# A fused conditional mixing and feed-forward kernel: its head rebuilt with a selector product, aggregation on VectorE per block, and other idle products

## The reference

```python
# x: (64, 32, 512), cond_128: (64, 128); K = 8 kernels
h = gelu(cond_128 @ W0 + b0)
h = gelu(h @ W1 + b1)
att = softmax(h @ W2 + b2)                        # (64, 8)
agg_w = einsum('bk,koi->boi', att, weight)        # one 32x32 matrix for each batch row
agg_b = att @ bias_k
hs = einsum('boi,bih->boh', agg_w, x) + agg_b[:, :, None]
routing = top_k(hs @ gate_w, 2)                   # over 8 logits; their two largest
shared = relu(hs @ up_w) ** 2 @ down_w            # 512 -> 1024 -> 512
routed = ((hs @ fc1_w) @ expert_w) * sum(routing) @ fc2_w
out = x + layernorm(shared + routed) * ln_gamma + ln_beta
```

## Time and profile before

| | us |
|---|---|
| median of 3 runs | 268.63 |
| lowest, highest | 267.57, 270.42 |
| span of the profiled execution | 266.2 |
| TensorE busy in it | 259.0 |
| VectorE, ScalarE, GpSimd busy | 154.9, 85.2, 44.6 |

### The profile page before, as it was taken

The page is one execution under the profiler, slowest core; times in us unless marked ns, Lnnn a source line. Parts: engine busy times, 40 slices in busy tenths (PEclk is TensorE's granted clock), DMA queues, the critical chain, the costliest instruction groups (busy, mean ns, idle before and its releaser), DMA issues.

```text
span 266.2 us, 3377 instructions
## 1 busy us (share of the span) xinstructions
PE 259.0 (97%) x1222; PEld 215.7 (81%) x1222; DVE 154.9 (58%) x268; ACT 85.2 (32%) x146; POOL 44.6 (17%) x42
## 2 busy tenths in 40 slices
PE   7999999999999999999999999999999999999991
PEld 7698888788888888888888888888888888778891
DVE  3686899974444954384544963384444963314454
ACT  4356994441111354241110354231110355211110
POOL 1000409101111800001111810001111700001111
PEclk9999999999999999999999999999999999999997
DMA  6973710400111240000111140000111100001111
GB/s 211 342 224 147 264 52 10 151 0 0 42 39 39 49 151 0 0 0 4 39 39 39 42 155 0 0 0 0 39 39 39 42 0 0 0 2 39 39 39 39
DMA packets 9132, 15.71 MB, mean 59 GB/s; under 512 B 634, under 2 KB 3578, under 8 KB 9122
## 3 DMA queue, kind: packets, MB, share of 16 engines
q1 hardware_dynamic: 9122, 15.57, 17.4%
HBM read 11.37 MB, written 4.20 MB: 58 GB/s over the span
## 4 chain that ended last, share of the span: by engine, by line
PE 95%; issue 2%; DVE 1%; POOLq 0%; POOL 0%; DVEq 0%
PE ps L774 26%; PE ps L776 26%; PE ps L775 26%; PE ps L760 6%; PE ps L714 2%; PE ps L719 2%; PE ps L838 1%; PE ps L840 1%; PE ps L746 1%; PE ps L850 1%; POOLq L80 0%; POOL rstd L378 0%; PE ps L755 0%; DVE stats L617 0%; DVE y_buf L615 0%
## 5 line engine op out<-in xcount | busy, mean ns | idle before, releaser
L774 PE MATMUL ps<-down_hi,sq_hi 128*128 128x512 f32 (+1 forms) x136 | 51.3, 377 | 0.0
L775 PE MATMUL ps<-down_lo,sq_hi 128*128 128x512 f32 (+1 forms) x136 | 51.2, 377 | 0.0
L776 PE MATMUL ps<-down_hi,sq_lo 128*128 128x512 f32 (+1 forms) x136 | 51.2, 377 | 0.0
L774 PE MATMUL ps<-h_hi,up_hi 128*128 128x512 f32 x128 | 50.3, 393 | 0.0
L776 PE MATMUL ps<-h_hi,up_lo 128*128 128x512 f32 x128 | 49.8, 389 | 0.0
L775 PE MATMUL ps<-h_lo,up_hi 128*128 128x512 f32 x128 | 49.8, 389 | 0.0
L378 POOL TENSOR_TENSOR rstd<-mv,half 128x1 f32<-128x1 f32 x16 | 15.7, 982 | 177.4 <-DVE mv L622 171.9
L456 ACT ACTIVATE relu_sq<-ps 128x512 f32<-128x512 f32 x32 | 19.1, 597 | 58.1 <-PE ps L776 44.2
L615 DVE TENSOR_TENSOR y_buf<-ps,y_buf 128x512 f32<-128x512 f32 x15 | 10.4, 691 | 45.9 <-PE ps L776 45.9
L589 DVE CAST sq_hi<-relu_sq 128x512 fp32r<-128x512 f32 x32 | 23.6, 737 | 20.9 <-ACT relu_sq L458 20.2
L473 ACT ACTIVATE y_buf<-ps,top 128x512 f32<-128x512 f32 x16 | 11.0, 689 | 69.2 <-PE ps L776 67.2
(11 more groups left out here) (105 smaller groups left out, 302.4 us busy)
## 6 DMA issues: line engine op xcount, KB each, us to landing
x_cur<-in_x_dram SPq DMA_DIRECT2D x4, 1024.0 KB, 5.5
out_dram<-late SPq DMA_DIRECT2D x15, 256.0 KB, 2.0
late<-in_up_w_dram SPq DMA_DIRECT2D x4, 512.0 KB, 10.0
late<-in_down_w_dram SPq DMA_DIRECT2D x4, 512.0 KB, 5.3
experts_sb<-in_experts_dram SPq DMA_DIRECT2D x1, 768.0 KB, 5.1
agg_b<-aggb_dram SPq DMA_DIRECT2D x1, 768.0 KB, 8.1
latents_sb<-in_latents_dram SPq DMA_DIRECT2D x1, 528.0 KB, 3.9
affine_sb<-in_affine_dram SPq DMA_DIRECT2D x1, 512.0 KB, 5.4
```

The costliest lines, as they stand in the source:

```text
L774: nc.tensor.matmul(dst, a_hi, b_hi, start=first, stop=False)
L775: nc.tensor.matmul(dst, a_hi, b_lo, start=False, stop=False)
L776: return nc.tensor.matmul(dst, a_lo, b_hi, start=False, stop=last)
```

## The change

Four things are changed in the head, and one in all blocks.

- The idle products load and move a 128x128 tile of ones (L757 of the new file), 37 of them instead of 26.
- The weights come with a strided load of 32 partitions on ScalarE's queue. VectorE transposes them in 32x32 blocks, one product with a repeated identity spreads them to 128 partitions, and VectorE copies them to `weight_T`. The attention is laid out by tile and spread to the same partitions by a product with a selector (ATT_P). Then VectorE multiplies the two (128x1024) and sums over k: that is the aggregate of one block, already on the partitions where `mix` needs it, so that four copies make `mix`.
- Block 0's bias is prepared by GpSimd and ScalarE and added by TensorE, as one product of ones with the bias parts into each mixing bank. `mix_bias` is gone from block 0; `h_hi` and `h_lo` are taken from PSUM.
- up_w is loaded in five pieces, the first ahead of x. The second and third mixing chunks move behind the first chunk of the up product, and two foldings move ahead of the mixing.
- The copies of the whole aggregate are gone. `next_aggregate(b)` on VectorE, behind the eight square splits of block b, computes the aggregate of block b + 1, and `next_mix` on GpSimd waits for it.

```diff
-    UPC = INT // 4
+    UP_COLS = [(0, 1), (1, 1), (2, 2), (4, 2), (6, 2)]
-    MIX0_BANK = [7, 4, 7, 4]
+    MIX0_BANK = [5, 4, 7, 5]
...
         @block.gpsimd
+            pool.wait_ge(bias_loaded, 16)
+            pool.wait_ge(attT_copied, 1)
+            nc.gpsimd.tensor_tensor(
+                att_bias.rearrange("k (b o) -> k b o", o=C),
+                att_T[:, 0:TOK // C].unsqueeze(2).to_broadcast([K2, TOK // C, C]),
+                bias_raw.unsqueeze(1).to_broadcast([K2, TOK // C, C]),
+                ALU.mult).then_inc(attb_ready, 1)
+            pool.wait_ge(attb_hi_ready, 1)
+            nc.gpsimd.tensor_tensor(bias_parts[LO, :], att_bias[LO, :], bias_parts[LO, :].bitcast(fp32),
+                                    ALU.subtract).then_inc(attb_lo_ready, 1)
...
-            pool.wait_ge(agg_act, 2 * G)
-            pool.wait_ge(agg_dve, 2 * G)
             def next_mix(b):
                 pool.wait_ge(mix_done, HC * (b + 1))
                 pool.wait_ge(xbeta_ready, b + 1)
+                pool.wait_ge(next_agg_ready, b + 1)
...
         @block.scalar
+            act.dma_start(weight_raw[:, :, :], weight_v).then_inc(weight_loaded, 16)
+            act.dma_start(bias_sb[:, :], kernels[0:K2, C * C:]).then_inc(bias_loaded, 16)
...
-            for q in (0, 1):
-                for g in range(G):
-                    nc.scalar.copy(mix_part(g, q), agg_src(q, g, TB)).then_inc(mix0_act, 1)
+            for g in (0, 1):
+                r = slice(g * C, (g + 1) * C)
+                nc.scalar.copy(mix[r, :, r], agg[r, 0:TB, :]).then_inc(mix0_act, 1)
...
         @block.vector
+            nc.vector.memset(idle[:, :].bitcast(mybir.dt.uint32), ONE_BITS).then_inc(dve_const, 1)
...
+            dve.wait_ge(weight_loaded, 16)
+            nc.vector.transpose(weight_t[:, :, :].rearrange("i k o -> i (k o)"),
+                                weight_raw[:, :, :].rearrange("o k i -> o (k i)")).then_inc(weight_t_ready, 1)
...
+            nc.vector.tensor_copy(weight_T[:, :, :], WEIGHT_T.rearrange("p (k o) -> p o k", o=C)
+                                  ).then_inc(weightT_copied, 1)
...
+            nc.vector.tensor_tensor(
+                first_terms, weight_T[:, :, :].unsqueeze(1).to_broadcast([P, TB, C, K]),
+                ATT_P[:, 0:TB, :].unsqueeze(2).to_broadcast([P, TB, C, K]), ALU.mult).then_inc(first_terms_ready, 1)
+            dve.wait_ge(first_terms_ready, 1)
+            nc.vector.tensor_reduce(agg[:, 0:TB, :], first_terms, AX.X, ALU.add).then_inc(first_agg_ready, 1)
...
+            def first_mix_low(c):
+                dve.wait_ge(h_hi_ready, c + 1)
+                nc.vector.tensor_tensor(h_lo[:, c, :], ps[:, MIX0_BANK[c], :], h_hi[:, c, :].bitcast(fp32),
+                                        ALU.subtract).then_inc(h_lo_ready, 1)
+
+            def next_aggregate(b):
+                if isinstance(b, int) and b == 0:
+                    dve.wait_ge(attP_copied, 1)
+                    dve.wait_ge(mix0_act, 2)
+                else:
+                    dve.wait_ge(mix_ready, G * b)
+                nc.vector.tensor_tensor(
+                    next_terms, weight_T[:, :, :].unsqueeze(1).to_broadcast([P, TB, C, K]),
+                    att_P[:, bass.ds((b + 1) * TB, TB), :].unsqueeze(2).to_broadcast([P, TB, C, K]),
+                    ALU.mult).then_inc(next_terms_ready, 1)
+                dve.wait_ge(next_terms_ready, b + 1)
+                nc.vector.tensor_reduce(agg[:, bass.ds((b + 1) * TB, TB), :], next_terms, AX.X, ALU.add).then_inc(next_agg_ready, 1)
...
-            for q in (2, 3):
-                for g in range(G):
-                    nc.vector.tensor_copy(agg_part(g, q), agg_src(q, g, NT)).then_inc(agg_dve, 1)
...
+            next_aggregate(0)
             latent_low(0)
...
         @block.tensor
-                    nc.tensor.matmul(IDLE, gate_hl[:, 0, :], gate_hl[:, 1:3, :], start=True, stop=True)
+                    nc.tensor.matmul(IDLE, idle[:, :], idle[:, :], start=True, stop=True)
...
-            for c in range(C // G):
-                last = nc.tensor.matmul(AGG[:, c, :], weight_parts[:, c * P:(c + 1) * P], att_parts[:, :],
-                                        start=True, stop=True)
...
+            def first_mix_chunk(c):
+                for t in range(TB):
+                    nc.tensor.matmul(ps[:, MIX0_BANK[c], t * P:(t + 1) * P], x_cur[:, t, c * P:(c + 1) * P],
+                                     mix[:, t, :], start=(t == 0), stop=False)
+                if c == 0:
+                    pe.wait_ge(attb_lo_ready, 1)
+                nc.tensor.matmul(ps[:, MIX0_BANK[c], :], ones[:, :], bias_parts,
+                                 start=False, stop=True).then_inc(mix_done, 1)
```

More of the change, by code:

```diff
@@ L41, in adaln_ffn_kernel @@
     K = mlp.shape[1] - NB - 2 * D - 2
-    SR = kernels.shape[0]
-    FIRST, LAST = slice(0, K), slice(SR - K, SR)
+    LO, K2 = slice(0, K), 2 * K
+    ONE_BITS = 0x3F800000
     INT = up_w.shape[1]
@@ L143, in adaln_ffn_kernel @@
         b1_sb = mlp_sb[:, NB + 2 * D + K + 1:NB + 2 * D + K + 2]
[L144 to L147, removed]
+        weight_raw = h_full[0:C, 0, 0:K * C].rearrange("o (k i) -> o k i", k=K)
+        weight_t = h_full[0:C, 1, 0:K * C].rearrange("i (k o) -> i k o", k=K)
+        repeat = sb("repeat", [C, G, C])
+        weight_T = sb("weight_T", [P, C, K])
+        bias_sb = sb("bias_sb", [K2, C + K])
+        bias_raw = bias_sb[:, 0:C]
+        idle = sb("idle", [P, P], f32r)
+        b2_sb = bias_sb[0:1, C:C + K]
+        sel_g = sb("sel_g", [NB, G])
+        sel = sb("sel", [NB, G, C])
+        in_tile = sb("in_tile", [NB, NT])
+        att_tiles = sb("att_tiles", [NB, NT, K])
+        att_P = sb("att_P", [P, NT, K])
         hid1 = sb("hid1", [D, NB])
@@ L165, in adaln_ffn_kernel @@
         logits = sb("logits", [P, TB, NE])
-        ones = sq_lo[0:2 * K, 1, 0:P]
+        ones = sq_lo[0:K2, 1, 0:P]
         half = sb("half", [P, 1])
@@ L172, in adaln_ffn_kernel @@
         H2 = ps[:, 4, 128:128 + NB]
[L173 to L177, removed]
+        LOGIT = ps[0:NB, 2, 0:K]
+        ATT_T = ps[0:K2, 4, 256:256 + NB]
+        ATT_P = ps[:, 3, 0:NT * K].rearrange("p (t k) -> p t k", k=K)
+        WEIGHT_T = ps[:, 5, 0:K * C]
+        IDLE = ps[:, 0, 0:P]
+        AGGB_ROWS = ps[0:NB, 2, 0:C]
         TOP = ps[:, TOP_BANK, 0:TB * 2 * NE].rearrange("p (t s n) -> p t n s", t=TB, s=2)
         Q = [ps[:, 6, :], ps[:, 7, :]]
[L182 to L192, removed]
         def shared(t):
@@ L205, in adaln_ffn_kernel @@
         mlp_loaded = sem("mlp_loaded")
-        kernels_loaded = sem("kernels_loaded")
+        weight_loaded = sem("weight_loaded")
+        bias_loaded = sem("bias_loaded")
         experts_loaded = sem("experts_loaded")
         x_loaded = sem("x_loaded")
-        up_loaded = [sem(f"up_loaded{i}") for i in range(4)]
+        up_loaded = [sem(f"up_loaded{i}") for i in range(len(UP_COLS))]
         latents_loaded = sem("latents_loaded")
@@ L688, in _ @@
                     split_square(b, m)
+                next_aggregate(b)
                 latent_low(b)
@@ new lines, in _ @@
+            nc.tensor.matmul(LOGIT, ones[0:1, 0:NB].bitcast(fp32), b2_sb, start=True, stop=False)
+            stay_warm(2)
+            pe.wait_ge(gelu_done, 2)
+            nc.tensor.matmul(LOGIT, hid2[:, :], w2_sb, start=False, stop=True).then_inc(logit_done, 1)
+            pe.wait_ge(weight_t_ready, 1)
+            pe.wait_ge(repeat_ready, 1)
+            nc.tensor.matmul(WEIGHT_T, repeat[:, :, :].rearrange("j g i -> j (g i)"),
+                             weight_t[:, :, :].rearrange("i k o -> i (k o)"),
+                             start=True, stop=True).then_inc(weightT_done, 1)
@@ L748, in _ @@
-            last.then_inc(agg_done, 1)
             pe.wait_ge(attT_copied, 1)
             nc.tensor.matmul(AGGB_ROWS, att_T[0:K, :], bias_raw[0:K, :], start=True, stop=True).then_inc(rows_done, 1)
-            stay_warm(1)
-            pe.wait_ge(attb_lo_ready, 1)
-            nc.tensor.matmul(AGG_B, ones[:, :], bias_parts, start=True, stop=True).then_inc(aggb_done, 1)
-            stay_warm(3)
+            fold_expert(0, 1, 0)
+            fold_expert(0, 1, 1).then_inc(q_done, 1)
+            stay_warm(6)
```

219 lines of the change are left out of this document (110 added, 109 removed).

## The result

The changed kernel took 278.77 us (median of 6, 275.60 to 280.77) against 268.75 (median of 6, 267.21 to 270.42). The ratio of the compared runs is 1.027, 95% interval 1.020 to 1.034. It is lower than the ratio of the medians because the comparison leaves out the three runs at 280.7 as disturbed; runs of two further kernels with this head, further down, fall into the same two groups, some 4 us apart. The prediction was 270.5 with a range of 266.3 to 272.6; all six times lie above it. The six times stand in groups: 275.6 twice, 276.84, and 280.7 three times. The profile is of one at 280.77, so it shows the worst group.

A forecast was written before the change was run, and what follows sets the result against it. TensorE, busy 259.0 of 266.2 us, was taken as the bound, so the head pays only by starting the up product earlier. Sum: 267.6 - 2.2 (head) + 3.5 (gap) + 0.1 (loop) + 1.5 (clock) = 270.5; range 266.3 to 272.6.

The forecast's parts named there:

- With the clock up: ... the up product starts at 15.4: Head, mixing to up product: at 2.4 GHz the first up product starts at 15.4 instead of 18.24 us, 2.8 earlier.
- the head's net gain of 2.2: Head: 2.8 us earlier start less 0.9 given back in the up product; 1.9, or 2.7 without GpSimd's hold; 2.2 taken.
- Idle products at 0.13, bound 0.19: Head start: twenty idle products at 0.13 us each by columns, at most 0.19; first real product at 3.5.
- Aggregate ready at 11.2, and the mixing on VectorE's chain: Head: VectorE's multiplication (1.26) and sum (1.2) end at 11.2 us; mixing follows its copies, at 11.9, or 12.8 if held.
- The clock up for the mixing: Head: TensorE at 2.4 GHz when mixing starts, so two chunks cost 0.11 us an instruction instead of 0.21.
- My rival for it: Head: idle products don't raise the clock; net gain only 0.5, total 270.7 to 272.2, about 271.6 us; chance 0.18.
- Bias product 0.23 each: Block 0 mixing: the bias becomes one 512-column product a chunk, 0.23 us each.
- GpSimd's hold of 0.8: Head: GpSimd's bias subtraction (1.2 us) holds VectorE's copies, so mixing starts at 12.8, gaining 0.8 instead of 1.7.
- The gap: End of block 0: TensorE waits 3.5 to 4.3 us, say 3.9, for the next aggregate and GpSimd's copies; net 3.5.
- The clock in the gap: Behind block 0's gap: the clock probably drops, costing 1.5 us (0 to 3.5); rival that it holds, 269.0, chance 0.25.
- The loop: Later blocks: aggregate and copies on time or slightly late, 0 to 0.3 us a block, 0.1 for both.

The follow-up runs named there:

- the early aggregate: Changed kernel with block 0's next_aggregate ahead of the eight square splits instead of behind: 273.86 us, ratio 1.016; control repeat 272.15, ratio 1.010.
- old idle products: Changed kernel with the idle products of before (96 columns of zero weights, 192 moved), 11 instead of 20 at the start: 272.71 us; with the early aggregate too, 269.53.
- old idle, 16 rows: Changed kernel with the early aggregate and the old idle products, bias products left at 16 rows: 269.53 us, ratio 0.999.
- 128 rows: Changed kernel with block 0's bias products padded from 16 to 128 rows: 276.55 us alone, 270.91 with the early aggregate.
- all three edits: Changed kernel with the early aggregate, the old idle products and bias products of 128 rows: 267.47 us, ratio 0.993.
- another kernel's: Changed kernel with only the bias products widened to 128 rows, gap and new idle products kept: 276.55 us, profiled execution 276.84.

## Why the prediction was wrong

**The step that failed is "With the clock up: ... the up product starts at 15.4", and with it the head's net gain of 2.2.** The second half started 8.2 us later instead of 2.2 earlier, 10.4 in all, where the profiled execution (280.77) missed the forecast by 10.3. The other terms nearly cancel: 0.9 less for gap and fall, 0.2 more in the other blocks, and 0.5 more outside the span. Of the 10.4, the mixing began 4.6 late (17.42 against 12.8), mixing to up product took 2.6 more (5.2), and the first half of the up product 2.9 more than the prediction's 14.9; the last 0.3 is the 2.2 taken where the terms gave 1.9. In the lower group too, with the clock up before the up product, the head is some 4 us late instead of 2.2 early (second half at 36.27 in the trace of the early aggregate, at 272.02). Its terms:

- *Idle products at 0.13, bound 0.19.* They cost 0.23. I let the price follow the columns moved and left the weights out; even my upper bound was too low. The mean weight load takes 0.33 us against 0.27 in the heads of the two kernels, and the products stand in the same ratio, 1.2; but no run varied the weights' columns alone, and the tile's values changed with them. H1 started at 5.6 instead of 3.5. In time: 2.6 us (269.53 against the lower group's 272.1), or 3.4 (267.47 against 270.91), the earlier rise of the clock included.
- *Aggregate ready at 11.2, and the mixing on VectorE's chain.* With H1 back at 3.56 (old idle products) the sum still ended at 12.7. I had left out the product that spreads the weights (L780, 1.15 us on the chain) and the four idle products behind it. The multiplication and the sum, 1.22 each, were right (1.26 and 1.2 predicted). And I never followed TensorE's own list to the mixing: it ended at 17.42, the copies at 16.80.
- *The clock up for the mixing.* Not so in this execution: low until 27.4. My rival for it priced only 1.1 us of mixing and no up product; a late rise cost 4.2.
- *Bias product 0.23 each.* That is the price at 128 rows. At 16 rows it was 0.43, and 0.2 more on what follows. The first half of the up product was 15.62 (old idle, 16 rows) and 14.80 (128 rows) instead of 13.97: 1.65 and 0.8 given back, where 0.9 was predicted.
- *GpSimd's hold of 0.8.* Right for the copies, 1.0 measured by taking it away, but the mixing waited for TensorE's list and not for them; its removal gained nothing.

Even with all three edits the second half starts at 32.03 against 32.21 in the profiled executions, 0.2 earlier and not 2.2; block 0's mixing, 2.84 instead of 3.26, is the rest of the 0.6 between their spans. By the medians that version gains 2.0 (267.47 against 269.47): the profiled execution of before, at 267.57, is one of its fastest. Where its slower ones lose their 1.9 us no trace shows.

**The gap was right in mechanism and near in size.** Predicted 3.9, measured 2.98. Shifted by the head's 10.4, TensorE was ready at 58.96 (58.8 predicted) and VectorE's last split ended at 57.96 (57.5 predicted). GpSimd's four copies took 1.33, not 2.3 to 2.95; that is most of the difference. That it costs 3.5 in all, without a fall of the clock, is shown by the early aggregate; gap and fall together cost 4.4 (276.3 to 280.7), 5.0 predicted.

**The clock in the gap** was put at 1.5. Against a mixing of 2.92 it cost 1.4 in the profiled execution, 2.5 in another kernel's, and nothing in the one with old idle products. The size was right as a middle, and the event is not certain.

**The loop** cost nothing (0.1 predicted); the other blocks are 0.3 longer.

The steps from all three edits (267.5) back to the lower group (275.6), 2.1 for the rows, 2.6 for the idle products and 3.5 for the gap, add up by construction. Two kernels outside that row test them: old idle products with the gap kept should come at 269.5 + 3.5 = 273.0 and came at 272.7; 128 rows with the gap kept and no fall at 275.6 - 1.2 = 274.4 to 275.6 - 2.1 = 273.5, and the one such time was 273.5.

**What stays open.** Why the narrow products went with a late rise only beside the new idle form: with the old one there was none in 16 times. And what decides in one execution whether the clock falls in a gap of 3.0 us. Neither was separated further, and no run has a shorter or a longer gap.

## What to carry to other kernels

Price a small product by a row of the same form, and by what stands around it: one with few rows among full ones cost 0.43 us instead of 0.23, and padding it with zeros made it cheaper. Work moved off a precomputed path into a block has to be placed where its engine waits, not just ahead of its user: the same two VectorE instructions cost 3.5 us at one place and nothing at the other. Before a head is credited with a gain, follow every engine's list through it, TensorE's idle products included, price each product by its row at the clock that this stretch really has, and take the times of several executions as data: groups 4 us apart were the first sign of a clock that rises by chance.

## What was not expected of the hardware

- A 512-column product of 16 rows among products of 128 rows took 0.43 us at 2.4 GHz and 0.72 at 1.2; with 128 rows 0.23 and 0.43. The products behind it took 1.09 for eight instead of 0.89.
- An idle product of 128 columns with 128 columns of weights (ones) cost 0.23 to 0.24 us at 1.2 GHz, one of 192 with 96 of weights (zeros) 0.19.
- TensorE was busy 21.55 of the first 22.61 us and still at 1.2 GHz; without any idle product, busy less, the clock rose in the first up product, at 17.97.
- In the traces a gap of 2.96 to 2.99 us left the clock up once (mixing 2.92) and dropped it three times (4.33, 4.37, 5.46).
- GpSimd's 8x512 subtraction made two VectorE copies last 1.48 us instead of 0.47, and was itself 1.70 instead of 1.26 beside a 128x512 VectorE subtraction.
